# GpSimd's low parts moved within a head of a fused two-layer transformer kernel

## The reference, cut to what matters

```python
x = x + attn0(layernorm(x))      # 16 heads of 128 for each of 2 batches
x = x + ffn0(layernorm(x))       # 16 routed experts, top 4, and a shared one
# attn0, for each batch and head:
q, k = rotary(xn @ W_Q + b_Q), rotary(xn @ W_K + b_K);  v = xn @ W_V + b_V
s = where(causal, q @ k.T / sqrt(128), 0)
m = max(abs(s));  w = sign(s) * exp(sign(s) * s - m)
out += (w / (sum(abs(w)) + 1e-6)) @ v @ W_O
```

## Time and profile before

| | |
|---|---|
| runs of the kernel before | 869.87, 874.43, 875.94 us, median 874.43 |
| profiled execution | 869.21 us, its span 867.5 us |
| TensorE, busy | 826.4 us, 95% |
| VectorE | 670.3 us, 77% |
| ScalarE | 522.9 us, 60% |
| GpSimd | 469.1 us, 54% |
| granted TensorE clock | 0.996 of full speed |

### The profile page before, as it was taken

One profiled execution on the slowest core, in us unless ns is written; L12 is line 12 of the kernel. 1 busy time (PEld: TensorE's weight loads), 2 busy tenths in 40 slices (PEclk: granted clock), 3 DMA queues, 4 the chain that ended last, 5 costly groups with the idle time before them and its releaser, 6 DMA issues.

```text
span 867.5 us, 14790 instructions
## 1 busy us (share of the span) xinstructions
PE 826.4 (95%) x4549; PEld 626.9 (72%) x4549; DVE 670.3 (77%) x1350; ACT 522.9 (60%) x1106; POOL 469.1 (54%) x399
## 2 busy tenths in 40 slices
PE   8899999999989999889998999999999989999997
PEld 6678888777878888667787888664444447888886
DVE  5799999999999999998477865868788644675554
ACT  3778888786878888763644533336566665454442
POOL 3565555665666666532575766614210526656774
PEclk9999999999999999999999999999999999999999
DMA  4323332222432223211665457412441133334451
GB/s 148 101 97 99 98 97 97 96 83 73 148 97 99 97 97 98 68 48 49 201 226 166 140 164 271 155 57 63 142 136 53 56 99 92 122 122 141 152 161 65
DMA packets 57426, 99.20 MB, mean 114 GB/s; under 512 B 8272, under 2 KB 19024, under 8 KB 57360
## 3 DMA queue, kind: packets, MB, share of 16 engines
q1 hardware_dynamic: 57360, 98.39, 35.6%
HBM read 71.88 MB, written 9.57 MB: 94 GB/s over the span
## 4 chain that ended last, share of the span: by engine, by line
PE 63%; DVE 11%; issue 10%; POOL 9%; ACT 4%; DMA 2%; DVEq 0%; SPq 0%; ACTq 0%; POOLq 0%
PE ps L956 10%; PE ps L942 9%; PE ps L933 9%; PE ps L319 6%; PE ps L382 5%; PE ps L330 4%; POOL q_sin L518 3%; PE ps L343 3%; PE ps L370 3%; PE ps L1505 3%; PE ps L1624 3%; PE ps L357 2%; DVE w L505 2%; PE ps L1594 2%; DVE nm L1816 2%
## 5 line engine op out<-in xcount | busy, mean ns | idle before, releaser
L1080 POOL TENSOR_TENSOR ew_lo<-ew_raw,ew_hi 128x768 fp32r<-128x768 f32 x68 | 128.1, 1884 | 64.5 <-ACT ew_hi L1046 46.0
L1032 ACT ACTIVATE hid_hi<-guw 128x512 fp32r<-128x512 f32 x68 | 43.0, 632 | 156.6 <-POOL guw L1096 106.5
L1135 DVE TENSOR_TENSOR hid_lo<-guw,hid_hi 128x512 fp32r<-128x512 f32 x68 | 80.6, 1185 | 72.4 <-ACT hid_hi L1032 72.3
L1096 POOL TENSOR_TENSOR guw<-gu,cwb 128x512 f32<-128x512 f32 x61 | 80.4, 1319 | 91.5 <-issue 74.0
L505 DVE SCALAR_TENSOR_TENSOR w<-ex,rden,sgn 128x512 f32<-128x512 f32 (+3 forms) x128 | 103.2, 866 | 0.0
L1816 DVE TENSOR_REDUCE nm<-ps 128x1 f32<-128x512 f32 x128 | 81.3, 682 | 19.9 <-PE ps L1528 18.7
L1711 ACT ACTIVATE e<-ps 128x512 f32<-128x512 f32 x128 | 68.7, 602 | 36.8 <-PE ps L1624 36.6
L518 POOL TENSOR_TENSOR q_sin<-q_sw,sin 128x512 f32<-128x512 f32 x64 | 85.6, 1354 | 3.0 <-DMA q_sw<-q_in 2.7
L433 ACT ACTIVATE ex<-sabs,nmax 128x512 f32<-128x512 f32 (+3 forms) x128 | 61.5, 552 | 36.3 <-DVE nmax L479 36.3
L956 PE MATMUL ps<-ew_hi,hid_hi 128*128 128x256 f32 x272 | 78.4, 288 | 2.4 <-DVE hid_lo L1135 1.8
L956 PE MATMUL ps<-ew_hi,hid_lo 128*128 128x256 f32 x272 | 76.9, 283 | 0.0
(11 more groups left out here) (189 smaller groups left out, 2443.4 us busy)
## 6 DMA issues: line engine op xcount, KB each, us to landing
ew_raw<-in_ew SPq DMA_DIRECT2D x68, 384.0 KB, 3.4
q_sw<-q_in SPq DMA_DIRECT2D x128, 128.0 KB, 2.0
cwb<-cw_dram SPq DMA_DIRECT2D x61, 256.0 KB, 3.6
wqk_raw<-in_wqk SPq DMA_DIRECT2D x32, 256.0 KB, 2.9
wv_raw<-in_wv SPq DMA_DIRECT2D x32, 128.0 KB, 2.7
wo_raw<-in_wo SPq DMA_DIRECT2D x32, 128.0 KB, 2.2
qs<-stk_q SPq DMA_DIRECT2D x16, 256.0 KB, 3.7
ks<-stk_k SPq DMA_DIRECT2D x16, 256.0 KB, 4.3
```

The source lines that it names most:

```text
L1080: pool.tensor_tensor(ff[f].ew[1][:, i % EW_SLOTS, :], ew_raw[:, i % RAW_SLOTS, :], fp(ff[f].ew[0][:, i % EW_SLOTS, :]), ALU.subtract).then ...
L1096: pool.tensor_tensor(ff[f].guw[:, i % 2, :], ff[f].gu[:, i % 2, :], ff[f].cwb[:, r % CWB_SLOTS, :], ALU.mult).then_inc(sem("guw"), 1)
L1135: dve.tensor_tensor(ff[f].hid[1][:, i % 2, :], ff[f].guw[:, i % 2, :], fp(ff[f].hid[0][:, i % 2, :]), ALU.subtract).then_inc(sem("hid_lo"), 1)
```

## The change

GpSimd's wqk_lo becomes a function of its own, wqk_low. In steps below 0 it stays first in the step. From step 0 on it comes behind the two affine selects. The ew_lo of steps 28 to 30 come directly behind it, without the wait for rden and ahead of wo_lo instead of behind wv_lo. wo_lo of head i waits for the denominators of head i+1. The wqk_lo of step -3 and the wv_lo of step -4 (head 0) wait for the first four xn.

```diff
-        def a0_pool(pool, i):
+        def wqk_low(pool, i):
             if valid(i + 3, N0):
                 n = i + 3
+                if known(i) and i == -3:
+                    pool.wait_ge(sem("xn"), QT)
                 wait(pool, "wqk_hi", n + 1)
                 pool.tensor_tensor(wqk[1][:, :, :, :], wqk_raw[:, :, :, :], fp(wqk[0][:, :, :, :]),
                                    ALU.subtract).then_inc(sem("wqk_lo"), 1)
+
+        def a0_pool(pool, i):
+            if known(i) and i < 0:
+                wqk_low(pool, i)
             if valid(i + 2, N0):
                 n = i + 2
                 for t in range(2):
...
                     pool.affine_select(out=diag, in_=diag, compare_op=ALU.is_ge, fill=0.0, base=0,
                                        pattern=[[0, QT], [-1, P]], channel_multiplier=1).then_inc(sem("causal"), 1)
+            if not known(i) or i >= 0:
+                wqk_low(pool, i)
+            if known(i) and N0 - 4 <= i <= N0 - 2:
+                ew_low(pool, 0, i - (N0 - 4))
             if valid(i, N0):
                 n = i
                 wait(pool, "wo_hi", n + 1)
+                if valid(i + 1, N0):
+                    wait(pool, "den", QT * (n + 2))
                 pool.tensor_tensor(wo[1][:, :], wo_raw[:, :], fp(wo[0][:, :]), ALU.subtract).then_inc(sem("wo_lo"), 1)
             if valid(i + 4, N0):
                 n = i + 4
                 wait(pool, "wv_hi", n + 1)
+                if known(i) and i == -4:
+                    pool.wait_ge(sem("xn"), QT)
                 pool.tensor_tensor(wv[1][:, slot_of(4), :, odd(), :], wv_raw[:, :, :], fp(wv[0][:, slot_of(4), :, odd(), :]),
                                    ALU.subtract).then_inc(sem("wv_lo"), 1)
...
-            if N0 - 4 <= i <= N0 - 2:
-                pool.wait_ge(sem("rden"), i + 2)
-                ew_low(pool, 0, i - (N0 - 4))
             if i == N0 - 2:
                 ew_low(pool, 0, 3)
```

## The result

The changed kernel takes 896.71 us (median of 6 runs, 891.24 to 899.32) against 875.18 for the kernel before (6 runs, 869.87 to 882.43): a ratio of 1.0246, 95% interval 1.0204 to 1.0287. It is slower by some 21 us; 888 was predicted, in a range of 874 to 902. The profiled execution went from 869.21 to 895.27 us, +26.1, where the working had +16.2 for it.

The account below looks back on a forecast made before the run. TensorE was taken as the bound in steady heads, 11.04 us each. Terms +19.6, +0.3, -0.4 and -3.3 sum to +16.2, giving 885.4 from the profiled execution or 890.6 from the median; 888 us predicted, range 874 to 902.

Parts of the forecast that it names:

- (a): Steady heads: moving wqk_lo off VectorE's w releases about 1.0 us per head, worth at most 7 us.
- the ring: Per-step loop: wqk_lo, wqk_raw and wv_raw loads, wv_hi, q_in, swap, q_sin, selects, wqk_lo again; taken as 12.0 us.
- (b): Steps 1 to 29: wv_raw's load waits behind wqk_lo, so steps take 12.0 us and TensorE waits; +19.6 us.
- (c): Step 0: first wqk_lo behind the selects ends at 42.64, delaying L319 of step 1; +0.3 us.
- (e): Start: head 0's wv_lo and wqk_lo wait for the first four xn, so transposes come earlier; -0.4 us.
- (d): Each head: wo_lo waits for the next head's denominators, wv_lo falls on w; cost 0, bounds 0 to 0.3 per head.
- (f): Steps 28 to 30: expert low parts ew_lo leave w, shortening its stretch; -3.3 us, bounds 0 and -6.
- Rival 1: Steady heads: faster, the ring doesn't bind and VectorE's relief is left; 858.5 us at TensorE's 11.04; chance 0.10.
- Rival 2: Steady heads: no measurable change, the ring binds at 11.4 to 11.7 us; 874 at 11.6; chance 0.12.
- rival 3: Steady heads: slower still, blocking at the GpSimd/VectorE port only moves; 899 at a ring of 12.5; chance 0.13.

Follow-up runs that it names:

- experiment 4: Kernel before with SP's wqk_raw and wv_raw loads swapped, wv_raw first, as a control: 873.45 us against 873.06, ratio 0.9996.
- experiment 11: Kernel before with the three expert weight loads spread one per step over steps 16 to 18, nothing else: 872.69 us against 873.1, ratio 0.9998.
- experiment 2: Changed kernel with SP's two loads swapped, wv_raw issued ahead of wqk_raw: 868.6 us against 873.06 for the kernel before, ratio 0.9972.
- experiment 6: Changed kernel with the three expert weight loads issued one per step, nothing else: 889.68 us against 871.69 for the kernel before, ratio 1.0216.
- experiment 1: Kernel before with only wqk_lo moved behind the selects from step 0 on: 896.43 us against 873.06, ratio 1.0279.
- experiment 7: Experiment 2 without wo_lo's wait for the denominators: 870.53 us against 871.69 for the kernel before, ratio 1.0003.
- experiment 3: Changed kernel with wqk_lo back at the head of the step, all else as changed: 877.92 us against 873.06 for the kernel before, ratio 1.0072.
- experiment 10: Experiment 3 without wo_lo's wait for the denominators: 870.34 us against 873.1 for the kernel before, ratio 0.9940.
- experiment 9: Changed kernel with two buffers for wqk_raw, SP's order untouched: 871.38 us against 871.69 for the kernel before, ratio 0.9992.

## Why the prediction was right or wrong, point by point

The ledger, for the profiled executions: start of step 1, start of step 29, the start of the matmuls of step 31 for an expert's gate (L933 before, L944 after), the end.

| stretch | before, us | after, us | difference | predicted |
|---|---|---|---|---|
| to L319 of step 1 | 42.44 | 43.07 | +0.6 | -0.1 |
| steps 1 to 29 | 316.44 | 340.93 | +24.5 | +19.6 |
| step 29 to the gate of step 31 | 38.75 | 37.65 | -1.1 | -3.3 |
| the rest | 469.87 | 471.95 | +2.1 | 0 |

One execution differs from the next. Experiments 4 and 11, whose GpSimd order is the old one and whose medians are those of the kernel before, take 319.1 and 318.5 us for steps 1 to 29, so a good 2 us of the +24.5 may be no more than that.

- **(a), right.** TensorE was the bound in the steady heads, so VectorE's relief could buy little. w went from 866 to 703 ns in the mean of 128 (21 us in all), L357's waits for w all but vanished, and where the ring is cut (experiment 2) the whole change stands at 0.9972 (0.9937 to 1.0008).

```profile
L505 DVE SCALAR_TENSOR_TENSOR w<-ex,rden,sgn 128x512 f32<-128x512 f32 (+3 forms) x128 | 82.4, 703 | 0.0
```

- **(b), the mechanism right, the size a little short.** 28 steps average 340.93 / 28 = 12.18 us instead of 12.0. Without the two long ones (13.59 and 15.72) the other 26 average 11.99. That this is so near 12.0 is in part luck, since several terms were off and cancelled. In the mean of these 26 rounds wv_hi starts 2.59 us after the issue of wv_raw, not 2.77. The groups of four swap issues that the earlier trace rows led me to expect at 3.53 didn't come (2.54 is the longest), so the +0.17 for them is nothing. Against these stand the gap between the end of wqk_lo (104.20) and the issue of wqk_raw (104.36), 0.16 or more in the looped heads where I took 0.01, the way from wv_hi to q_in, 0.38 instead of 0.31, and that from the first swap issue to q_sin, 2.71 instead of 2.61, both in the mean. In the head shown it is 3.10 (111.46 - 108.36), which is the longest of the 26.
- **(b), where TensorE loses it.** I had all of it ahead of L319, about 1 us a head. The profile puts 8.7 us there, 5.9 of them in the two long steps, and 7.6 us at L357 behind sgn, which I hadn't named. The length of the step is as forecast, since it is the ring's.
- **(b), what was missed.** The 15.72 is 3.7 us over the ring. The working had the loads of a head in SP's queue and not the expert loads that stand there once, in step 16. In the kernel before, the swap was issued 4 us after them; the ring moved the swaps to 0.5 us behind them. Experiment 6 shows that step at 12.09 once they are spread. The 13.59 has a late landing of wo_raw (3.4 us) and of a swap (3.7) in it, and its cause stays open.
- **(c) right, (e) right in the first half, open in the second.** The first wqk_lo behind the selects went as worked out, and at the start L319 of head 0 came 0.58 earlier (13.38 against 13.96). But wv_raw of head 1 and the second rstd were later, and in this execution xn of the second half met wqk_lo and took 2.39 where the earlier trace rows have 1.38:

```profile
16.80 2.39 DVE L242 TENSOR_SCALAR xn<-x,meanvar,rstd 128x256 f32<-128x256 f32 x4 [2.20 <-POOL rstd L265]
17.77 1.26 POOL L513 TENSOR_TENSOR wqk_lo<-wqk_raw,wqk_hi 128x512 fp32r<-128x512 f32 x1 [1.01 <-ACT wqk_hi L398]
```

Experiment 6 has the same instructions up to there. Its xn starts 0.10 earlier and its wqk_lo 0.06 later, and it is wqk_lo that takes longer:

```profile
16.70 1.38 DVE L242 TENSOR_SCALAR xn<-x,meanvar,rstd 128x256 f32<-128x256 f32 x4 [2.04 <-POOL rstd L265]
17.83 1.38 POOL L513 TENSOR_TENSOR wqk_lo<-wqk_raw,wqk_hi 128x512 fp32r<-128x512 f32 x1 [1.17 <-ACT wqk_hi L398]
```

Step 1 starts at 42.27 there and at 43.07 in the profiled execution of the changed kernel, against 42.44 before. So the +0.6 of the ledger is one execution's; experiment 6 has -0.2, where -0.1 was forecast.

- **(d), right in the ring, wrong outside it.** Experiments 1 and 7, in which wqk_lo has moved, find no price for the wait for the denominators; experiments 3 and 10, in which wqk_lo still has to meet w, find 1.3%. The working named a cover, a step of 12 us. Experiments 2 and 7, with and without the wait, show no difference at steps of 11.04 us either, so with wqk_lo out of the way of w the cover wasn't needed.
- **(f), mis-sized.** The stretch got shorter by 1.1 us, not by 3.3, here and in experiment 6 alike (37.65 us in both). ew_lo did leave w, which takes 2.95 in step 28 instead of 5.23. But the ex product that it met took 2.20 instead of 0.55, and xn, which now runs beside the two q_sin, the selects and the next ew_lo, 4.46 instead of 2.00:

```profile
384.42 2.20 DVE L486 SCALAR_TENSOR_TENSOR ex<-sgn,ex 128x384 f32<-128x384 bf16 x1
...
388.79 2.95 DVE L505 SCALAR_TENSOR_TENSOR w<-ex,rden,sgn 128x512 f32<-128x512 f32 x4
391.66 4.46 DVE L242 TENSOR_SCALAR xn<-x,meanvar,rstd 128x256 f32<-128x256 f32 x4
```

I followed the stretch of one instruction and not where GpSimd's next ones would land. With wqk_lo in its old place the same move of ew_lo does give 2.6 and 3.1 us (experiments 3 and 10).

- **The rest, +2.1.** The expert layers and the second attention have the same instructions. In the traces of experiments 1 to 4, 6, 7, 10 and 11 this part takes 469.2 to 473.7 us, in no order that follows the change, so I don't put the 2.1 down to it.
- **The rivals.** Rival 1 (the ring doesn't bind) is what experiments 2 and 9 make of the kernel. They came out at 0.997 and 0.999 and not at the 858.5 us that I gave it, since the stage doesn't fall to 28 steps of 11.04 us, which is 309.1: it takes 317.4 us in the trace of experiment 2 and 314.6 in that of experiment 9. In experiment 2 the steps at the expert loads are 14.99 and 12.63 long; in the second of them TensorE is busy throughout at a granted clock of 0.86. In experiment 9 it is three steps of 12.7 us in which VectorE is busy throughout and L358 (the L357 of that kernel) waits 1.5 us for w: there VectorE is the bound, which the steady heads hadn't shown. Rival 2 (a ring of 11.4 to 11.7) falls with the 11.99 measured, rival 3 with experiments 1 and 2.
- **The choice between two bases** (885.4 from the profiled execution, 890.6 from the median): the medians are the better base, as one profiled execution can be 6 us off its median, and the middle gave away half of the difference. From the median alone the forecast would have been 890.6, against 896.71.

## What to carry to other kernels

When an instruction moves later on one engine, follow every wait on its semaphore, and behind each of those everything that stands in the same queue. Here a DMA queue held a wait for the moved instruction, an unrelated load stood behind that wait, and a third engine stood on that load ahead of the instruction that starts the next round. A chain like that costs nothing until its length passes the bound of the stage, so add it up from the rows before moving anything: 5 us of distance between a load and its use is slack only as long as the load's own wait stays where it is. Loads whose own wait is long satisfied go ahead of loads that have to wait.

## What the runs showed that I had not expected

- A swap DMA of 2.0 us lands after 3.8 to 6.1 us when 1.15 MB of other loads were issued within the 2 us before it (expert loads at 237.84, swaps at 239.69).
- VectorE's xn, a tensor_scalar with one tensor input in SBUF, is held up beside GpSimd's products as those with two inputs are: 4.46 and 2.39 us against 1.38. In the two rows at 16.80 and 16.70 a tenth of a microsecond at the start went with a change of the engine that loses.
- A gap of 1.91 us on TensorE ahead of L319, at the end of the step that took 13.59, is followed by matmuls of 0.63 us where 0.39 is usual, and by a whole L319 group of 4.58 where 2.78 is usual. The granted clock was 0.52 from 81 to 84 us, the lower of its two levels, 1.2 GHz, and 0.86 in the mean of the step, 79.98 to 92.58. The gap of 3.97 in the long step did the same, and so did one of 3.69 in experiment 2 (0.86 in the mean of its step) and one of 2.20 among the transposes in experiment 1 (0.62 in the 2.5 us behind it). The gaps of up to 1.0 us in the other heads did not, nor did those of 1.04 and 1.59 in experiment 1. The two steps that open at the lower level, 12.60 and 12.53 us long, end in an L319 that waits for nothing: there TensorE was the bound again, some 0.6 us above the ring. In the other heads the ring didn't slow TensorE's clock as well.
